# A decoder block on one core: one expert scatter moved between POOL's builds, two ScalarE steps exchanged, the router's setup moved into the first step

## The reference

```
x = x + attn(layernorm(x))            # A: 16 heads of 8, rope, phi = elu + 1, causal linear attention
x = x + xattn(layernorm(x), ctx, ctx) # B: 16 heads of 8, softmax(q k^T / sqrt(8)) v, with a mask
x = x + ffn(layernorm(x))             # C: shared SwiGLU expert + 2 of 8 routed SwiGLU experts per token

def ffn(x):
    xn = layernorm(x) * ln_scale + ln_bias      # for the router alone
    probs = softmax(xn @ gate_w.T)
    tk_probs, tk_idx = top_k(probs, 2); tk_probs /= sum(tk_probs) + 1e-5
    out = swiglu(x, sWg, sWu, sWd)              # x is the layernorm of the line above
    for e in range(8):
        out += w[:, e:e+1] * swiglu(x, Wg[e], Wu[e], Wd[e])
```

## Time and profile before

| what | value |
|---|---|
| timed runs, median (lowest to highest) | 992.42 us (991.8 to 996.79), 3 runs |
| profiled execution, its own time | 982.63 us |
| its span | 980.8 us |
| PE busy in the span | 783.7 us, 80% |
| DVE busy | 693.7 us, 71% |
| ACT busy | 571.9 us, 58% |
| POOL busy | 567.3 us, 58% |
| mean granted TensorE clock | 0.93 |

### The profile page before, as it was taken

The page is one execution under the profiler, slowest core; times in us unless marked ns, Lnnn a source line. Parts: engine busy times, 40 slices in busy tenths (PEclk is TensorE's granted clock), DMA queues, the critical chain, the costliest instruction groups (busy, mean ns, idle before and its releaser), DMA issues.

```text
span 980.8 us, 37069 instructions
## 1 busy us (share of the span) xinstructions
PE 783.7 (80%) x14483; PEld 610.8 (62%) x14483; DVE 693.7 (71%) x1705; ACT 571.9 (58%) x1185; POOL 567.3 (58%) x762
## 2 busy tenths in 40 slices
PE   3778886887887787797797786797999988989891
PEld 2556665665665565575575554685877777777670
DVE  2256787889888988989988786578455555556773
ACT  3467786866866776777776553452255444454450
POOL 5365554765875775766764575338135555555562
PEclk9799999998998998989998877998999999999996
DMA  9211101211220220220220201402212222225765
GB/s 242 56 46 46 46 16 44 58 51 31 60 65 16 57 66 17 59 62 17 62 59 20 65 21 29 136 14 58 58 49 75 75 74 75 79 72 162 199 193 165
DMA packets 96038, 68.54 MB, mean 70 GB/s; under 512 B 9680, under 2 KB 88027, under 8 KB 95872
## 3 DMA queue, kind: packets, MB, share of 16 engines
q1 hardware_dynamic: 84592, 47.95, 19.0%
q0 software_dynamic: 8640, 16.93, 5.2%
q10 hardware_dynamic: 2640, 1.31, 0.5%
HBM read 43.05 MB, written 24.02 MB: 68 GB/s over the span
## 4 chain that ended last, share of the span: by engine, by line
PE 57%; DVE 24%; issue 10%; ACT 7%; DMA 1%; POOL 1%; another core or an unknown queue 1%; POOLq 0%; SPq 0%; ACTq 0%; DVEq 0%
PE pair_x L857 8%; PE bank L875 7%; PE pair_x L572 6%; PE pair_x L662 4%; DVE c_hit L1564 4%; PE bank L488 4%; DVE mx L1468 3%; PE bank L679 3%; PE bank L608 3%; DVE Qblk L1430 3%; PE pair_x L738 2%; DVE Ex L1472 2%; PE bank L750 2%; PE pair_y L738 2%; PE bank L630 2%
## 5 line engine op out<-in xcount | busy, mean ns | idle before, releaser
L1371 POOL DMA_INDIRECT mixed<-f_y,f_x x142 | 139.5, 982 | 132.8 <-ACT f_y L1144 87.4
L1254 POOL DMA_INDIRECT routed<-c_row,c_idx x128 | 135.9, 1062 | 126.0 <-PE bank L679 74.5
L875 PEld LDWEIGHTS bank<-Qblk,Am 128*128 128x128 f32 x568 | 78.7, 190 | 49.4 <-issue 42.6
L875 PE MATMUL bank<-Qblk,Am 128*128 x568 | 92.4, 285 | 17.8 <-DVE Am L1787 14.3
L662 PE MATMUL pair_x<-con,Ex 128*128 128x128 f32 x512 | 76.4, 298 | 12.6 <-ACT Am L960 7.8
L989 ACT ACTIVATE Ex<-Ex 128x1024 f32<-128x1024 f32 x64 | 67.2, 1050 | 32.0 <-DVE Ex L1472 31.9
L1144 ACT ACTIVATE f_y<-bank,f_x 128x128 f32<-128x128 f32 x142 | 52.5, 370 | 56.4 <-PE bank L875 48.6
L572 PE MATMUL pair_y<-Kblk,KQ 32*64 32x256 f32 x1024 | 83.7, 449 | 0.0
L1139 ACT ACTIVATE qk<-pair_x 128x256 f32<-128x256 f32 x142 | 55.6, 391 | 46.5 <-PE pair_x L857 27.2
L995 ACT COPY ExT<-pair_x 128x1024 f32<-128x1024 f32 x64 | 64.3, 1005 | 30.6 <-PE pair_x L662 23.0
L1468 DVE TENSOR_REDUCE mx<-pair_y 128x16 f32<-128x1024 f32 x64 | 77.2, 1206 | 6.4 <-PE pair_y L572 4.8
(11 more groups left out here) (204 smaller groups left out, 2134.8 us busy)
## 6 DMA issues: line engine op xcount, KB each, us to landing
f_x<-routed SPq DMA_DIRECT2D x142, 65.0 KB
ctxD<-in_ctx SPq DMA_DIRECT2D x32, 256.0 KB
ctxP<-in_ctx SPq DMA_DIRECT2D x16, 256.0 KB
maskB<-in_mask_BxS_if SPq DMA_DIRECT2D x16, 256.0 KB
Cblk<-mixed SPq DMA_DIRECT2D x16, 256.0 KB
Kblk<-mixed SPq DMA_DIRECT2D x16, 256.0 KB
block_out<-X SPq DMA_DIRECT2D x11, 256.0 KB
mixed<-f_y,f_x POOLq DMA_INDIRECT x142
```

The source lines that it names most:

```text
L875: ins = pe.matmul(banks[F_O[n % 2]][:, 0:D], f_hT[:, u % 3, c * P:(c + 1) * P], wdn[:, bass.ds(e, 1), c, :].rearrange("p o d -> p (o d)"), ...
L1254: pool.indirect_dma_start(routed[:, :], bass.IndirectOffsetOnAxis(ap=c_idx[:, d % ROW_SLOTS, t, n:n + 1], axis=0), c_row[:, d % ROW_SLOTS, ...
L1371: pool.indirect_dma_start(mixed[:, :], bass.IndirectOffsetOnAxis(ap=f_x[:, u, D + 1:D + 2].bitcast(I32), axis=0), f_y[:, u, :], None, boun ...
```

## The change

Four things change; the arithmetic is the same.

- POOL: scatter 7 leaves its place behind scatter 6. It now follows K block 0 of h, behind a wait for b's first product; K blocks 1 and 2 come behind it.
- ACT: `a_norm(e)` (four operations) stands ahead of `c_norm_evac(c)` (one) instead of behind it.
- The router's setup: gate_w, ln_scale and ln_bias get a semaphore of their own, g_in. PE's weight transposes wait for four loads in place of seven. The gate's transpose, scaling, bias product and evacuation move into the step in which f = 0, around A's V projection on PE and ahead of the rotation on DVE.
- POOL's mask bias moves from ahead of the first root to behind the marks.

```
-            sp.dma_start(b_xn[0:E, 0, :], gate_w).then_inc(S["w_in"], 16)
+            sp.dma_start(b_xn[0:E, 0, :], gate_w).then_inc(S["g_in"], 16)
...
             pe.wait_ge(S["con_in"], 16)
-            pe.wait_ge(S["w_in"], 7 * 16)
+            pe.wait_ge(S["w_in"], 4 * 16)
             for n in range(4):
-                pe.transpose(banks[0][:, n * D:(n + 1) * D], a_xn[:, n, :], ident)
-            pe.transpose(banks[1][:, 0:E], b_xn[0:E, 0, :], ident[0:E, 0:E]).then_inc(S["set_ps"], 1)
-
-            pe.wait_ge(S["set_z"], 1)
-            pe.wait_ge(S["set_d"], SET_DVE)
-            pe.matmul(banks[1][:, E:2 * E], rot[:, 0:P], rot[:, P:P + E], start=True, stop=True).then_inc(S["set_ps2"], 1)
+                ins = pe.transpose(banks[0][:, n * D:(n + 1) * D], a_xn[:, n, :], ident)
+            ins.then_inc(S["set_ps"], 1)
             pe.wait_ge(S["set_cp"], 2)
+
+            def gate_T():
+                pe.wait_ge(S["g_in"], 3 * 16)
+                pe.transpose(banks[1][:, 0:E], b_xn[0:E, 0, :], ident[0:E, 0:E]).then_inc(S["set_gT"], 1)
+
+            def gate_bias():
+                pe.wait_ge(S["set_z"], 1)
+                pe.wait_ge(S["set_g"], 2)
+                pe.matmul(banks[1][:, E:2 * E], rot[:, 0:P], rot[:, P:P + E], start=True, stop=True)\
+                    .then_inc(S["set_ps2"], 1)
+                pe.wait_ge(S["set_d"], SET_DVE)
...
+                if f == 0:
+                    gate_T()
                 if on(f):
                     a_project_v(f)
+                if f == 0:
+                    gate_bias()
...
@@ ACT, step
+                if on(e):
+                    a_norm(e)
                 if on(c):
                     c_norm_evac(c, odd)
-                if on(e):
-                    a_norm(e)
...
@@ POOL, step
                 if sent:
                     values_of_a(a, 0)
-                    for k in range(6, GT * TOP):
-                        c_scatter(d - 1, odd, k)
+                    c_scatter(d - 1, odd, 6)
...
                 if on(h):
                     b_block(h, 0, odd)
+                if sent:
+                    values_of_b(b, 0)
+                    c_scatter(d - 1, odd, 7)
+                if on(h):
                     b_block(h, 1, odd)
                     b_block(h, 2, odd)
...
@@ POOL, ahead of the steps
-            pool.wait_ge(S["m_in"], 2 * 16)
-            pool.wait_ge(S["con_in"], 16)
-            share = const("share")
-            for n in range(C):
-                ins = pool.tensor_scalar(bias[:, :, n, :], mask_rows[:, :, :], 0.0, share[:, n:n + 1], ALU.is_equal, ALU.mult)
-            ins.then_inc(S["b_bi"], 1)
             pool.wait_ge(S["set_z"], SET_ZERO - 1)
             rsqrt(0, a_mv, a_rs, a_nm, S["a_ag"], S["a_pw"], S["a_rsd"], S["a_xnd"])
...
+            (the same bias lines, behind the marks)
...
@@ DVE
+            def gate_scaled():
+                dve.wait_ge(S["g_in"], 3 * 16)
+                dve.wait_ge(S["set_gT"], 1)
+                dve.wait_ge(S["set_z"], 1)
+                dve.tensor_scalar(gateT[:, :], banks[1][:, 0:E], lnp[:, 0:1], None, ALU.mult).then_inc(S["set_g"], 1)
+                dve.tensor_scalar(rot[:, P:P + E], banks[1][:, 0:E], lnp[:, 1:2], None, ALU.mult).then_inc(S["set_g"], 1)
+                dve.wait_ge(S["set_ps2"], 1)
...
+                if f == 0:
+                    gate_scaled()
                 if on(f):
                     a_rotate(f)
```

More of the change, by code:

```diff
@@ L81 @@
 B_LOADS = 4
-SET_ZERO, SET_DVE = 9, 9
+SET_ZERO, SET_DVE = 9, 7
 Y_RING = 4
@@ L277, in decoder_block @@
         y_in2 = Kblk[:].rearrange("p m s r n -> p (m s r n)")
-        names = """w_in x_in0 x_in1 x_in2 con_in s_in m_in ffw_in set_z set_ps set_cp set_ps2 set_d
+        names = """w_in g_in x_in0 x_in1 x_in2 con_in s_in m_in ffw_in set_z set_ps set_cp set_gT set_g set_ps2 set_gs set_d
             a_st a_ag a_pw a_rsd a_xnd a_xnT_ps a_xnTd a_qk_ps a_qkd a_v_ps a_vd a_r2 a_r1 a_mn a_ex a_ph
@@ L347, in _ @@
                 sp.dma_start(a_xn[:, n, :], w).then_inc(S["w_in"], 16)
-            sp.dma_start(b_xn[0:E, 0, :], gate_w).then_inc(S["w_in"], 16)
-            sp.dma_start(lnp[:, 0:1], ln_scale.rearrange("(d a) -> d a", a=1)).then_inc(S["w_in"], 16)
-            sp.dma_start(lnp[:, 1:2], ln_bias.rearrange("(d a) -> d a", a=1)).then_inc(S["w_in"], 16)
+            sp.dma_start(b_xn[0:E, 0, :], gate_w).then_inc(S["g_in"], 16)
+            sp.dma_start(lnp[:, 0:1], ln_scale.rearrange("(d a) -> d a", a=1)).then_inc(S["g_in"], 16)
+            sp.dma_start(lnp[:, 1:2], ln_bias.rearrange("(d a) -> d a", a=1)).then_inc(S["g_in"], 16)
             sp.dma_start(X[:, GT:X_FIRST, :], tok[:, GT:X_FIRST, :]).then_inc(S["x_in1"], 16)
@@ L543, in a_mask_first @@
                     pe.wait_ge(S["a_am"], NP * a + j)
+                else:
+                    pe.wait_ge(S["set_gs"], 1)
                 for i in range(2):
@@ L599, in a_values @@
                     if not since(a, 1):
-                        pe.wait_ge(S["set_cp"], 3)
+                        pe.wait_ge(S["set_gs"], 1)
                     pe.wait_ge(S["a_vd"], C * a + C)
@@ L901, in _, with gate_bias_evac @@
             act.copy(woT[:, :], banks[0][:, 3 * D:4 * D]).then_inc(S["set_cp"], 1)
-            act.wait_ge(S["set_ps2"], 1)
-            act.mul(gate_sum[:, :], banks[1][:, E:2 * E], -1.0).then_inc(S["set_cp"], 1)
+            def gate_bias_evac():
+                act.wait_ge(S["set_ps2"], 1)
+                act.mul(gate_sum[:, :], banks[1][:, E:2 * E], -1.0).then_inc(S["set_gs"], 1)
             def normalise(i, src, rs, nm, dst, s_rs, s_xn):
@@ L1071, in step @@
                     a_v_evac(f, odd)
+                if f == 0:
+                    gate_bias_evac()
                 if shared_of(s, 3) + 1 in range(GROUPS):
@@ L1365, in _ @@
             ins.then_inc(S["set_z"], 1)
+            pool.wait_ge(S["m_in"], 2 * 16)
+            share = const("share")
+            for n in range(C):
+                ins = pool.tensor_scalar(bias[:, :, n, :], mask_rows[:, :, :], 0.0, share[:, n:n + 1], ALU.is_equal, ALU.mult)
+            ins.then_inc(S["b_bi"], 1)
             steps(step)
```

5 lines of the change are left out of this document (removed).

## The result

The changed kernel took 950.85 us (median of 4 runs, 943.1 to 956.31) beside 992.11 for the kernel before (4 runs, 986.94 to 996.79): ratio 0.958, 95% interval 0.949 to 0.967, so about 41 us faster where 46 were forecast. A second comparison on another chip gave 893.31 beside 923.2 us, 30 us faster: ratio 0.965 (0.960 to 0.970).

A forecast was written before the change was run, and what follows sets the result against it. PE sets a step's first half, DVE the second, where c_hit waits for POOL's run of builds. The terms 39.4 (steps), 0.5 (ACT's order alone) and 5.9 (first step) sum to 45.8 us, rounded to 46, off 992.42; range 936 to 968.

The forecast's parts named there:

- The size: Whole kernel: 46 us less, rounded from a sum of 45.8 us.
- The steps: Attention steps: 3.9 us gained in most, 39.4 us together; steps of 31.5 to 33 us, PE's wait near 1 us.
- c_hit: DVE's index operation, s = 5 to 14: near 0.7 us in place of 3.87, ending behind POOL's third build.
- Rival 1: POOL goes from third build straight into the scatter, holding DVE off until build five; 984 us, chance 0.10.
- The swap: ACT's a_norm before c_norm_evac: worth nothing alone, but keeps ACT and PE out of the way once DVE is earlier.
- rival 2: Attention steps: c_hit short, but L1430 still meets POOL's build or ACT or PE ends the half; 957 us, chance 0.14.
- The end of the attention stage: Last attention steps: gains of 3.3 us in s = 14, 0.5 in s = 15, 2.2 in s = 16.
- The first step: Kernel's start: POOL's root first and fewer loads awaited, a_xn 6.0 us earlier; 5.9 after 0.1 for the moved gate work.
- Rival 3: Start: POOL's first computation cannot begin before 10.75, so 1.4 us gained in place of 6.0; 951 us, chance 0.12.
- Rival 4: Attention steps: POOL's new wait for B's first product delays its builds and scatter 0; 998 us, chance 0.06.

The follow-up runs named there:

- experiment 4: Changed kernel with scatter 7 moved behind all five of POOL's builds, so the run is whole again; 974.67 us, ratio 0.986 to the kernel before.
- experiment 1: Kernel before with only POOL's scatter 7 moved behind B's first product, ACT's order and first step unchanged; 978.21 us, ratio 0.989.
- Experiment 3: Kernel before with only the first step's change (router setup and mask bias moved); 986.0 us, ratio 0.996.
- experiment 10: Changed kernel with c_pos in PSUM and scatter 7 back ahead of POOL's five builds; 949.04 us, ratio 0.965 to the kernel before.
- experiments 10 and 11: The second of the two: experiment 10's kernel with DVE's routing weights put behind the two divisions; 952.86 us, ratio 0.972 to the kernel before.

## Why the prediction was right, point by point

- *The size.* 946 against 950.85, ratio 0.953 against 0.958. Right, but in part by luck: in the two profiles the lead at the first expert product is 36.5 us where my terms sum to 45.8, the steps up to s = 13 gave more than forecast and those behind them took some back. The second chip gave 30 us.
- *The steps.* At the c_hit of s = 13 the lead was 39.9 us. My terms up to there, with those of s = 13 still to come since they lie behind c_hit, sum to 35.9. Of the 4 us more, 2.2 were there at the c_hit of s = 5 (8.6 in place of 6.4). From there to the c_hit of s = 13 before took 288.07 us and after 256.81: 3.9 a step, where the sum had 3.7 on the mean (29.5 us for these eight, measured 31.3). Step lengths of 31.8 to 32.8 and PE's wait of 1.13 to 1.30 us are as named.
- *c_hit.* Named were 0.7 us and an end behind the third build. The end is right, the size wrong (1.96): the sum kept c_hit's issue where it was relative to the run, and it now comes earlier, in the second build. Since only its end decides, the gain stood. The weights start at once and are held (0.68 us) as named.
- *Rival 1, break not open:* refuted by the rows and by experiment 4.
- *The swap.* "Alone worth nothing" was 5 us short. That it "is what keeps ACT and PE out of the way" of the split fits experiment 1, which has rival 2's new wait in place. I had doubted it when I wrote expectation 1, and the prediction's own working was the better guide. But most of what experiment 1's eight steps lack lies in held rotations, which neither had.
- *The end of the attention stage.* Here a term failed. From the c_hit of s = 13 on I had 9.9 us more of gain (3.9 and 6.0); between it and the first expert product the lead fell from 39.9 to 36.5 us. Of this, the step up to the c_hit of s = 14 lost 2.0 (36.9 in place of 34.9 us) through the held rotation, 3.6 us that my sum did not have. I counted what leaves POOL's queue before the builds, and not that transfer 7 had kept a late DVE operation clear of them. The trace of before shows it: there the same rotation also came 0.38 us behind transfer 6 (504.00), and with transfer 7 next (505.34) it took 1.22 us. s = 15 gave 1.5, s = 16 lost 3.5 and s = 17 gave 2.6. In s = 16 the same thing happened to an operation of the router's second pick: 0.35 us behind transfer 6 in both kernels, it takes 0.19 us in before and 2.82 in the changed one, where the builds follow directly. That this hold of 2.6 us is most of the loss of 3.5 fits, but is argued and not tested. In before, and then in the changed kernel:

```profile
504.38 1.22 DVE L1408 TENSOR_TENSOR rot<-qk,con 128x1024 f32<-128x1024 f32 x1
...
568.84 0.19 DVE L1523 TENSOR_TENSOR c_hit<-c_hit,con 128x32 f32<-128x32 f32 x1
```

```profile
530.36 2.82 DVE L1550 TENSOR_TENSOR c_hit<-c_hit,con 128x32 f32<-128x32 f32 x1
```

- *The first step.* Forecast 5.9. ACT's a_xn came 6.5 us earlier (13.95 to 7.43) and the first c_hit 6.1, but the first scores only 4.8 (31.45 to 26.69), because PE then ran most of the transposes of q and k at the lower of its two clock levels, 1.2 GHz (0.21 us apart in place of 0.11; granted clock 0.88 from 9.2 to 26.7, 0.98 in the same work of before). Experiment 3 gives about 4 in the whole.
- *Rival 3, nothing at the start:* its mechanism is refuted. POOL's first root ran at 5.31. What the Trainium skill states for a first call (GPSIMD Engine Reference, 2.1, about 6 us) did not show.
- *Rival 4, slower:* its wait came, but late in the stage only: POOL waited for B's first product 1.63 us at 468.64, where the late rotation had put PE behind, 2.63 us at 535.75 behind the held pick, and 2.99 us at 564.28. In the steps up to s = 13 it did not wait there.

## What to carry to other kernels

Read a slow DVE operation against POOL's timeline: if its end follows the end of POOL's run and not its own start, ask which of its inputs could lie in PSUM before reordering a queue, since one edit of that kind gave what three edits of order gave here. When an item is taken out from between a queue's other items, list what ran in its shadow: here a late rotation and a late pick did. And price edits together: the split alone gave 1.1%, the whole 3.5 to 4.2%.

## What the runs showed of the hardware

*How long a DVE operation is held.* Where the builds follow directly on a transfer: until POOL's run of builds has ended, whichever build it was issued in. So it is for 1.96 and 3.95 us (c_hit, three and five builds) and 4.82 and 6.79 us (rotation, issued during the transfer in front), and for all held operations of these steps in the 14 profiles but one (c_hit at 178.33 in experiment 4, 0.87 us). It is not so in the run of builds in s = 4, before the first transfer to the experts' lists. There DVE's operations with two SBUF inputs get in between two builds, each ending within 0.1 us of one build's end while the next build follows at once, in every one of the 14 profiles. DVE and POOL in before (143.21 in the earlier trace rows belongs to the same run):

```profile
144.43 0.74 DVE L1525 TENSOR_TENSOR c_pick<-con,c_m 128x32 f32<-128x32 f32 x1
145.21 0.96 DVE L1536 TENSOR_TENSOR c_sel<-c_pick 128x32 bf16<-128x32 f32 x1
```

```profile
144.09 3.04 POOL L1203 TENSOR_TENSOR Kblk<-ctxT,con 128x512 f32<-128x512 f32 x3
```

The operation's size does not decide: the one of 143.21 is the one held for 2.82 us in s = 16 of the changed kernel. Whether the transfer in front does was not tested; no experiment put something between it and the builds.

*Which operation is held.* With builds directly behind transfer 6 the rotation was held all nine times that it came 0.37 to 0.39 us behind that transfer's start, was not held the one time that it came 0.15 us behind it (experiment 4, 175.01, 1.21 us), and never when it came 0.31 us or more ahead of it. With transfer 7 behind transfer 6, ten rotations came 0.37 or 0.38 us behind transfer 6, and all took 1.22 us. A fraction of a microsecond of order between two engines decides over 3.6 us.

*Scores that come late with the record at full clock.* Not expected and not settled. ACT's ReLU of the first scores (Am) starts 1.6 us after PE's first score product in seven of nine steps of the changed kernel on the second chip. In its first profile and in experiment 10, on other chips, it starts 2.9 to 3.9 us after it, also in steps with a granted clock of 1.00. PE and ACT of the changed kernel on the second chip, of experiment 10, and ACT of the changed kernel's first profile (its product is the row at 351.50 above):

```profile
277.91 0.39 PE L573 MATMUL pair_y<-bias,couple 64*128 64x512 bf16 x2 [1.51 <-DVE Ex L1499]
```

```profile
279.52 1.00 ACT L976 ACTIVATE Am<-pair_x 128x1024 f32<-128x1024 f32 x1
```

```profile
389.19 0.39 PE L573 MATMUL pair_y<-bias,couple 64*128 64x512 bf16 x2 [0.40 <-ACT KQ L999]
```

```profile
393.05 1.02 ACT L976 ACTIVATE Am<-pair_x 128x1024 f32<-128x1024 f32 x1 [2.25 <-remote]
```

```profile
354.50 1.02 ACT L976 ACTIVATE Am<-pair_x 128x1024 f32<-128x1024 f32 x1 [1.29 <-remote]
```

PE's idle time ahead of the product plus the time to Am is 1.25 + 3.00 = 4.25 us in the one and 0.40 + 3.86 = 4.26 in the other. For s = 5 to 13 of both profiles this sum is 4.20 to 4.28 us, 18 times. So on those chips a shorter wait of PE at this place came to nothing in experiment 10, whose PE waited for Am in place of DVE, while on the second chip the steps came down to 30.4 us. That this is also why experiments 10 and 11 won nothing is argued and not shown: none of them ran on the second chip. Part of it is the clock (in four of the changed kernel's nine steps the record has 0.50 there, and the product takes 0.61 us in place of 0.39), but the steps with the record at 1.00 have the same sum. The cause stays open.

*Chips.* The same kernel before took 923 us on one chip and 985 to 992 on others. In the changed kernel's profiles 40 of the 63 us between the second chip and the first comparison lie in the experts' stage (238.8 against 279.2 us).
